# Attention scores as one product of 96 stacked rows per head, with the stacks filled by DMA, on one core

## Chip, cores and metric

The kernel runs on 1 core of one Trainium2 chip. The metric is the device time of the program in microseconds (us). Three executions of the kernel before took 4857.65, 4858.83 and 4860.56 us.

## The reference

Four attention layers are applied to `x` of shape (4, 1024, 512), each as `x = x + layer(layernorm(x))`, with 16 heads of 32 channels and a causal mask:

```python
x = x + attn_a(layernorm(x))  # "squared": (q.k)^2, no softmax; q and k are normed per head; o/(sum+eps); Wo
x = x + ffn(layernorm(x))     # "gated": k and v are one head's share, picked per token by a gate; softmax
x = x + attn_b(layernorm(x))  # "mqa": one k, v for all heads; softmax; output projection with bias
x = x + ffn(layernorm(x))     # "gated" again
# gated:
att = einsum('bhqd,bkd->bhqk', q, k_shared) / sqrt(32)
att = softmax(where(causal, att, -inf)); y = einsum('bhqk,bkd->bhqd', att, v_shared)
```

## The kernel before, in words

There are two acts. The first does the squared layer for the four batch entries, the second the three softmax layers ("soft" in the names of buffers: gated, mqa, gated, each for four entries, so 12 stages). A stage has four phases `ph` of four heads (a head group: 4 x 32 channels on 128 partitions); the first act has 16 phases and the second 48.

A phase makes the scores of its four heads in ten **keys** bursts (`KEY_BURSTS`: keys on partitions, up to 512 queries along the row, the upper triangle left out in blocks of 128) and, in the second act, the scores of the phase that follows in ten **rows** bursts (`ROW_BURSTS`: the same scores with queries on partitions), of which only the row maxima are wanted. The maxima become a shift of the softmax: `mxr` (VectorE and GpSimd), `mxt` (TensorE transposes the maxima to a row, ScalarE takes them out). ScalarE turns the keys bursts into probabilities, GpSimd masks them (`affine_select`) and adds up the unmasked ones, and TensorE multiplies them with the values (`av`) and sums them (`sm`).

Queries and keys are kept as two rounded halves, HIGH and LOW (fp32r), and a score is the sum of three products of 32 rows each (`PAIRS`): high by high, high by low, low by high. The four heads lie in different row quarters of TensorE and their products run side by side, so a part of a burst is 12 matmuls in three groups of four. In the second act a keys part begins with four bf16 matmuls that put the shift into PSUM (line 1107), and a rows part on the diagonal ends with four bf16 matmuls that add the mask (line 1138). VectorE then takes the maximum of two heads in one `reduce_max` (line 885).

Scores live in six PSUM banks as three pairs of banks, used in turn; a burst uses two pairs, one for each two heads. `need_pairs` makes TensorE wait for both pairs of a burst before its first matmul, and both become complete at the burst's end. The other work uses two banks in turn (`work`).

The order of everything is one list of events (`plan`) that all engines walk, each doing its share. `phase` fixes the bursts and the `av`, `sm`, `mxr`, `mxt` events in 20 half steps a phase; `spread` fills the other products in between by their `WEIGHT` and by due times; long ones are halved (`more` events). `q`, `q2`, `k2` are products that make queries and keys, four f32 matmuls by 128 channels (eight instructions in the trace); `kvar` (L1228) is eight small matmuls on the squares of the keys, which GpSimd makes in two instructions (`ksq`, lines 696 and 697) after VectorE has written the LOW half. SyncE issues all DMAs in the list's order.

## Time and profile before

| | us |
|---|---|
| median of 3 runs | 4858.83 |
| the profiled execution's own time | 4860.0 |
| its span | 4858.0 |
| TensorE busy in the span | 4146.2 (85%) |
| VectorE, ScalarE, GpSimd busy | 1919.3, 1600.3, 1585.0 |
| first act, second act (first to last instruction, about) | 0 to 1204, 1204 to 4858 |
| DMA queue of SyncE, share of 16 engines | 7.3% |

The span is the stretch between first and last instruction; the time has about 2 us more. TensorE's busy time is a union of pipelined matmuls, so for the price of a piece of work the start of the next piece is read, not the busy time.

### The profile page before, as it was taken

The numbers are of one execution on the slowest core, as the hardware profiler recorded it, in microseconds if no ns is written. First come the engines' busy times: TensorE is split into PE (matmuls) and PEld (weight loads), VectorE is DVE, ScalarE is ACT, GpSimd is POOL, SyncE is SP. The second block draws the span as 40 slices with busy tenths as digits, with TensorE's granted clock in tenths as the row PEclk, the third lists the DMA queues.
The fourth block names the chain that finished last, engine by engine and source line by source line (L and its number), as shares of the span: only waits on it lengthen the run. The fifth ranks groups of instructions, "written<-read, shape, count | busy, mean of one in ns | idle before, by whom it ended". The sixth has DMA issues, their size and how long they took to land.

```text
span 4858.0 us, 85613 instructions
## 1 busy us (share of the span) xinstructions
PE 4146.2 (85%) x36898; PEld 1987.7 (41%) x36898; DVE 1919.3 (40%) x2850; ACT 1600.3 (33%) x1985; POOL 1585.0 (33%) x1703
## 2 busy tenths in 40 slices
PE   6799898996979889798888888888899897988886
PEld 4344444442434444444443334434444444444443
DVE  1222222222544444444444444344444444444442
ACT  1333333342133233333433333233332333333333
POOL 1322222221133332424443343343333324242343
PEclk8899999998989999999998999999999999999998
DMA  1001001012000100101010010100101001010010
GB/s 59 18 1 36 18 18 36 1 36 88 14 18 1 40 14 1 53 1 36 19 36 18 4 50 1 36 19 18 36 1 36 18 1 53 1 36 18 1 36 29
DMA packets 63442, 116.23 MB, mean 24 GB/s; under 512 B 8673, under 2 KB 9185, under 8 KB 63073
## 3 DMA queue, kind: packets, MB, share of 16 engines
q1 hardware_dynamic: 63072, 110.77, 7.3%
q8 instruction: 298, 4.88, 0.4%
q14 instruction: 72, 0.58, 0.0%
HBM read 77.19 MB, written 33.55 MB: 23 GB/s over the span
## 4 chain that ended last, share of the span: by engine, by line
PE 54%; DVE 8%; POOL 4%; ACT 4%; issue 4%; DMA 1%; POOLq 0%; DVEq 0%; ACTq 0%; SPq 0%
PE banks L1176 11%; PE banks L1078 9%; PE banks L1129 8%; PE banks L1071 7%; PE banks L1111 6%; DVE maxima_soft L885 5%; PE banks L1107 3%; ACT probs_soft L812 3%; POOL full_sum_soft L730 3%; PE banks L1275 2%; PE banks L1138 2%; PE banks L1250 1%; PE banks L1166 1%; PE banks L1185 1%; POOL tiles_soft L710 1%
## 5 line engine op out<-in xcount | busy, mean ns | idle before, releaser
L885 DVE TENSOR_REDUCE maxima_soft<-banks 128x2 f32<-128x1024 f32 (+3 forms) x1152 | 1040.9, 953 | 1120.3 <-PE banks L1138 821.1
L812 ACT ACTIVATE probs_soft<-banks 128x1024 f32<-128x1024 f32 (+1 forms) x960 | 889.6, 978 | 1299.1 <-PE banks L1111 1299.0
L720 POOL TENSOR_SCALAR_AFFINE_SELECT probs_soft<-probs_soft 128x512 f32<-128x512 f32 x384 | 239.0, 634 | 1188.9 <-ACT probs_soft L812 1188.4
L1129 PE MATMUL banks<-k_soft,q_soft 32*128 32x512 f32 (+2 forms) x6912 | 498.9, 391 | 67.5 <-ACT probs_soft L812 66.0
L1111 PE MATMUL banks<-q_soft,k_soft 32*128 32x512 f32 (+2 forms) x6912 | 525.6, 412 | 0.0
L730 POOL TENSOR_TENSOR full_sum_soft<-full_sum_soft,probs_soft 128x2048 f32<-128x2048 f32 x96 | 435.7, 4538 | 251.6 <-ACT probs_soft L812 251.3
L1176 PE MATMUL banks<-probs_soft,v_soft 128*32 128x512 f32 (+3 forms) x4608 | 450.0, 510 | 16.6 <-DVE scaled_out_soft L1022 11.7
L1129 PEld LDWEIGHTS banks<-k_soft,q_soft 32*128 32x128 f32 x6912 | 287.9, 192 | 373.0 <-issue 341.9
L812 ACT ACTIVATE probs_squared<-banks 128x1024 f32<-128x1024 f32 (+1 forms) x320 | 296.5, 978 | 391.5 <-PE banks L1111 305.8
L1107 PE MATMUL banks<-shift_soft,ones 32*128 32x512 bf16 (+2 forms) x2304 | 212.7, 356 | 171.0 <-DVE maxima_soft L885 167.1
L1111 PEld LDWEIGHTS banks<-q_soft,k_soft 32*128 32x128 f32 x6912 | 325.8, 196 | 17.7
L730 POOL TENSOR_TENSOR full_sum_soft<-probs_soft 128x2048 f32<-128x2048 f32 x48 | 217.7, 4536 | 350.0 <-issue 232.7
L1176 PE MATMUL banks<-probs_soft,ones 128*32 128x512 f32 (+3 forms) x3072 | 264.3, 464 | 62.9 <-ACT shift_soft L798 41.5
L1071 PE MATMUL banks<-xnT_soft,g_wq 128*128 128x512 f32 x512 | 249.7, 616 | 11.0 <-DVE q_soft L911 8.6
L1078 PE MATMUL banks<-g_wk,xnT_soft 128*128 128x512 f32 x512 | 255.5, 630 | 3.9 <-ACT y_soft L798 3.6
L1078 PE MATMUL banks<-g_wv,xnT_soft 128*128 128x512 f32 x512 | 247.4, 613 | 13.4 <-DVE sums_soft L985 9.7
L1107 PEld LDWEIGHTS banks<-shift_soft,ones 32*128 32x128 bf16 x2304 | 65.6, 92 | 412.1 <-issue 401.2
L1176 PEld LDWEIGHTS banks<-probs_soft,v_soft 128*32 128x32 f32 x4608 | 124.4, 112 | 260.4 <-issue 215.6
L720 POOL TENSOR_SCALAR_AFFINE_SELECT probs_squared<-probs_squared 128x512 f32<-128x512 f32 x128 | 79.7, 635 | 440.2 <-ACT probs_squared L812 440.2
L1185 PE MATMUL banks<-ident,tiles_soft 128*128 128x128 f32 x384 | 85.0, 365 | 131.4 <-POOL tiles_soft L710 130.7
L1111 PE MATMUL banks<-q_squared,k_squared 32*128 32x512 f32 (+2 forms) x2304 | 158.0, 386 | 22.9 <-ACT probs_squared L812 22.8
L1176 PEld LDWEIGHTS banks<-probs_soft,ones 128*32 128x32 f32 x3072 | 83.3, 112 | 198.9 <-issue 92.2
(160 smaller groups left out, 4751.3 us busy)
## 6 DMA issues: line engine op xcount, KB each, us to landing
tiles_soft<-out SPq DMA_DIRECT2D x96, 256.0 KB, 2.7
rest_soft<-out SPq DMA_DIRECT2D x96, 256.0 KB, 3.0
out<-rest_soft SPq DMA_DIRECT2D x96, 256.0 KB, 2.5
tiles_squared<-in_x SPq DMA_DIRECT2D x32, 256.0 KB, 2.7
rest_squared<-in_x SPq DMA_DIRECT2D x32, 256.0 KB, 2.9
out<-rest_squared SPq DMA_DIRECT2D x32, 256.0 KB, 2.0
raw_wq<-in_squared_wq SPq DMA_DIRECT2D x1, 1024.0 KB, 5.5
raw_wk<-in_squared_wk SPq DMA_DIRECT2D x1, 1024.0 KB, 7.7
```

The source lines that it names most:

```text
L720: ins = pool.affine_select(out=cells, in_=cells, compare_op=ALU.is_ge, fill=0.0, base=0, pattern=[[0, HG], [1, P]], channel_multiplier=-1)
L730: pool.tensor_tensor(m["full_sum"][:], before, slot(ph, n)[:], ALU.add).then_inc(sg.probs_added, 1)
L812: act.activation(slot(ph, n)[:, 2 * a:2 * a + 2, 0:width], score_pair(e, a)[:, :, 0:width], ACT.Exp if soft else ACT.Square, scale=SCALE). ...
L885: ins = dve.reduce_max(m["maxima"][:, ph % 2, 2 * a:2 * a + 2, t, p], score_pair(e, a)[:, :, col:col + P * blocks_seen(t, p, blocks)], AX_X)
L1071: ins = pe.matmul(out, wt[:, kc, cols], m["xnT"][:, kc, CHUNK * c:CHUNK * c + CHUNK], start=(kc == 0), stop=(kc == KC - 1))
L1078: ins = pe.matmul(out, m["xnT"][:, kc, P * t:P * t + P], wt[:, kc, cols], start=(kc == 0), stop=(kc == KC - 1))
L1107: pe.matmul(psum[:, score_bank(e, i), col:col + width], k["ones16"][D * i:D * i + D, :], m["shift"][D * i:D * i + D, ph % 2, c, q0:q0 + wi ...
L1111: ins = pe.matmul(psum[:, score_bank(e, i), col:col + width], k_of(ph)[D * i:D * i + D, a, P * kb:P * kb + P], q_of(ph)[D * i:D * i + D, b ...
L1129: ins = pe.matmul(psum[:, score_bank(e, i), col:col + P * blocks], q_of(ph)[D * i:D * i + D, a, P * t:P * t + P], k_of(ph)[D * i:D * i + D ...
L1138: ins = pe.matmul(psum[:, score_bank(e, i), last - P:last], k["ident16"][:], k["mask"][:], start=False, stop=True)
L1176: ins = pe.matmul(out[D * i:D * i + D, q0:q0 + width], left, slot(ph, n)[:, i, col:col + width], start=(x == 0 and (soft or u == "av" or p ...
L1185: ins = pe.transpose(tile_of(out, kc), tile_of(m["tiles"][:, tile_slot(s, t), :], kc), k["ident"][:])
```

## The change

1. A score is one product. For each head the rows of queries (HIGH, HIGH, LOW) and of keys (HIGH, LOW, HIGH) are stacked to 96 partitions, and one fp32r matmul of 96 rows gives the sum of the three products. In the second act keys bursts have 98 rows: two more rows of queries hold the shift's HIGH and LOW part against two rows of ones of the keys. The matmuls of L1107 and L1138 are gone. A part of a burst is four matmuls, two for each pair of banks, and TensorE waits for one pair at a time (`need_pair`).
2. The stacks are filled by DMA. ScalarE and VectorE write HIGH and LOW of a `q`, `q2` or `k2` into one of two buffers `pair`; SyncE copies them with 12 DMAs of 32 x 512 elements (64 KB) into one of three stacks of 512 columns; the shift takes four DMAs of 2 x 512. In the list these are the events `stack` and `shifted`. Keys of the second act are not copied: they are made four times over already and are written in place. The bf16 split of the maxima in three parts (five GpSimd instructions) becomes an fp32r split in two (two instructions), and the transposes of `mxt` are fp32r matmuls with the identity.
3. The causal mask of row scores is added by VectorE, for one head at a time, in a `tensor_tensor_reduce` that also takes the maximum.
4. The list is made anew: `av` and `sm` are no longer halved and stand at one place each; queries (and keys of the first act) are made later and by halves of the phase (`made`), `kvar` stands right behind `ksq`.

```diff
-PAIRS = [(HIGH, HIGH), (HIGH, LOW), (LOW, HIGH)]
+QUERY_ROWS, KEY_ROWS = (HIGH, HIGH, LOW), (HIGH, LOW, HIGH)
+STACKS = 3
+STACK = 3 * D
-VALUES_AT = {"C": 0, "A": 6, "B": 14}
+VALUES_AT = {"C": 1, "A": 7, "B": 15}
-HALVED = ("av", "sm", "q", "q2", "k2", "v2", "ks", "kall", "vall")
+HALVED = ("q", "q2", "k2", "v2", "ks", "kall", "vall")
 def features(ph):
-    return [(u, ph, c) for c in range(NC) for u in ("q2", "k2", "ksq")] + [("kvar", ph, c) for c in range(NC)] + [("vscale", ph)]
+    made = [[("q2", ph, c), ("qsq", ph, c), ("k2", ph, c), ("ksq", ph, c), ("kvar", ph, c)] for c in range(NC)]
+    return made[0], made[1] + [("vscale", ph)]
@@ phase
-        for u, first in (("av", h), ("sm", h + 2)):
-            pieces = in_halves([(u, of, part)], kinds)
-            for n, event in enumerate(pieces):
-                at[first + n].append(event)
+        at[h].append(("av", of, part))
+        at[h + 1 if part == "B" else h].append(("sm", of, part))
@@ plan, second act
+                return [(queries(kinds[s + g // NG], 4 * s + g)[c], HALVES * (g - 2) + 6 * c, HALVES * (g - 1) - 2 + 6 * c)]
@@ stacked: where the DMAs stand in the list
+        if e[0] in ("q", "q2", "k2"):
+            u, ph, c = e
+            number = NC * ph + c - STACKS
+            old, chunk = divmod(number, NC)
+            waiting.append((("stack", e), ("keys", old, ends[u[0], chunk]) if number >= 0 else None))
+        elif e[0] == "mxt":
+            placed.append(("shifted", e))
+        elif e[0] == "keys":
+            passed.add(e)
+        while waiting and (waiting[0][1] is None or waiting[0][1] in passed):
+            placed.append(waiting.pop(0)[0])
@@ SyncE
+                elif u == "stack":
+                    wait_free(sp, made)
+                    if number >= STACKS:
+                        sp.wait_ge(sg.keys_scored, 2 * (of_kind["keys", old, last] + 1))
+                    for i in range(HG):
+                        for x, a in enumerate(QUERY_ROWS if name[0] == "q" else KEY_ROWS):
+                            sp.dma_start(stack[D * x:D * x + D, number % STACKS, i, :].bitcast(F32),
+                                         pair_of(made)[D * i:D * i + D, a, :].bitcast(F32))\
+                                .then_inc(sg.stacked[moved[made] % 2], DMA)
@@ ScalarE, before it writes HIGH
+                        if moved[e] >= 2:
+                            wait_stack(act, old)
@@ VectorE
+                            if p < t // TPC:
+                                ins = dve.reduce_max(...)
+                                continue
+                            for x in range(2):
+                                scores = score_pair(e, a)[:, x, col:col + width]
+                                ins = dve.tensor_tensor_reduce(scores, scores, k["mask"][:, CHUNK - width:CHUNK], 1.0, MASKED, ALU.add,
+                                                               ALU.max, m["maxima"][:, ph % 2, 2 * a + x, t, p:p + 1])
@@ TensorE, keys (rows are alike)
-                    need_pairs(e)
-                    for kb, q0, width, col in parts:
-                        if soft:
-                            for i in range(HG):
-                                pe.matmul(psum[:, score_bank(e, i), col:col + width], k["ones16"][D * i:D * i + D, :],
-                                          m["shift"][D * i:D * i + D, ph % 2, c, q0:q0 + width], start=True, stop=False)
-                        for x, (a, b) in enumerate(PAIRS):
-                            for i in range(HG):
-                                ins = pe.matmul(...)
+                    rows = STACK + 2 if soft else STACK
+                    for a in range(2):
+                        need_pair(e, a)
+                        for kb, q0, width, col in parts:
+                            for i in (2 * a, 2 * a + 1):
+                                ins = pe.matmul(psum[:, score_bank(e, i), col:col + width], k_stack(ph, i, P * kb, P, rows),
+                                                q_stack(ph, c, i, q0, width, rows), start=True, stop=True)
+                        ins.then_inc(sg.keys_scored, 1)
```

Three places show how the list moves instructions. In these listings an f32 product stands as `x4` where the trace has eight instructions, and the shape is that of the output.

First, TensorE in the first act, where the keys of the second phase (`k2`, s_wk) and their variances (L1228, now L1318) are made between the first bursts. Before:

```order
L1071 MATMUL banks<-xnT_squared,s_wk 128x512 x2
L1111 MATMUL banks<-q_squared,k_squared 128x512 x12
L1176 MATMUL banks<-probs_squared,v_squared 32x512 x4
L1176 MATMUL banks<-probs_squared,v_squared 32x384 x4
L1071 MATMUL banks<-xnT_squared,s_wk 128x512 x2
L1176 MATMUL banks<-probs_squared,v_squared 32x256 x4
L1176 MATMUL banks<-probs_squared,v_squared 32x128 x4
L1228 MATMUL banks<-head_mean,key_square_squared 128x4 x4
```

Of the change:

```order
L1178 MATMUL banks<-xnT_squared,s_wq 128x512 x4
L1215 MATMUL banks<-q_stack_squared,k_stack_squared 128x384 x4
L1178 MATMUL banks<-xnT_squared,s_wk 128x512 x4
L1318 MATMUL banks<-head_mean,key_square_squared 128x4 x4
L1215 MATMUL banks<-q_stack_squared,k_stack_squared 128x256 x8
```

The variances now follow the product of the same keys with nothing on TensorE in between; before, half an `av` stood there (and at other places whole bursts).

Second, TensorE in the second act from the last keys burst of the fifth phase (the two parts 256 wide) over the next rows and keys bursts to the first rows burst of the phase after next. Before:

```order
L1111 MATMUL banks<-q_soft,k_soft 128x256 x12
L1129 MATMUL banks<-k_soft,q_soft 128x512 x12
L1138 MATMUL banks<-mask,ident 128x128 x4
L1107 MATMUL banks<-shift_soft,ones 128x512 x4
L1111 MATMUL banks<-q_soft,k_soft 128x512 x12
L1176 MATMUL banks<-probs_soft,v_soft 32x512 x4
L1176 MATMUL banks<-probs_soft,v_soft 32x384 x4
L1071 MATMUL banks<-xnT_soft,g_wq 128x512 x4
L1176 MATMUL banks<-probs_soft,v_soft 32x256 x4
L1176 MATMUL banks<-probs_soft,v_soft 32x128 x4
L1071 MATMUL banks<-xnT_soft,g_wq 128x512 x4
L1185 MATMUL banks<-ident,tiles_soft 128x128 x8
```

Of the change, down to the same rows burst (L1228, 256 wide) and the `av` behind it:

```order
L1228 MATMUL banks<-k_stack_soft,q_stack_soft 128x512 x4
L1215 MATMUL banks<-q_stack_soft,k_stack_soft 128x256 x8
L1228 MATMUL banks<-k_stack_soft,q_stack_soft 128x512 x4
L1215 MATMUL banks<-q_stack_soft,k_stack_soft 128x512 x4
L1178 MATMUL banks<-xnT_soft,g_wq 128x512 x4
L1228 MATMUL banks<-k_stack_soft,q_stack_soft 128x256 x8
L1266 MATMUL banks<-probs_soft,v_soft 32x512 x4
```

Between the last keys burst and the rows burst of new queries stand two bursts and one product now, and the two `av` pieces have become one behind that rows burst; four bursts follow each other with nothing between.

Third, SyncE in the second act, one phase's worth. Before, it had only the loads and stores of tiles there:

```order
L681 DMA out<-rest_soft 128x512 [waits summed]
L673 DMA rest_soft<-out 128x512 [waits stored0]
L681 DMA out<-rest_soft 128x512 [waits summed]
L673 DMA rest_soft<-out 128x512 [waits stored1]
L681 DMA out<-rest_soft 128x512 [waits summed]
```

Of the change, where no tile is loaded or stored:

```order
L737 DMA q_stack_soft<-shift_soft 2x512 [waits work_free1]
L737 DMA q_stack_soft<-shift_soft 2x512 x3
L730 DMA q_stack_soft<-pair_soft 32x512 [waits keys_scored,work_free0]
L730 DMA q_stack_soft<-pair_soft 32x512 x11
L737 DMA q_stack_soft<-shift_soft 2x512 [waits work_free0]
L737 DMA q_stack_soft<-shift_soft 2x512 x3
L730 DMA q_stack_soft<-pair_soft 32x512 [waits keys_scored,work_free1]
L730 DMA q_stack_soft<-pair_soft 32x512 x11
```

A stack's 12 DMAs wait until the keys bursts that read the stack's former contents have been scored.

## Rows read from the trace of the kernel before

**Rows 1.** Page, part 1: busy us of each engine (share of the span), instructions.
```profile
PE 4146.2 (85%) x36898; PEld 1987.7 (41%) x36898; DVE 1919.3 (40%) x2850; ACT 1600.3 (33%) x1985; POOL 1585.0 (33%) x1703
```
**Rows 2.** Waits of TensorE: who waited for whom, us in total, times, longest.
```profile
PE banks L1107 <- DVE maxima_soft L885: 167.1, 195, 4.7
...
PE banks L1129 <- ACT probs_soft L812: 66.0, 66, 1.3
...
PE banks L1228 <- POOL key_square_squared L697: 31.3, 10, 3.4
```
**Rows 3.** Timeline of TensorE, bursts between other work: start, us, instructions.
```profile
3021.38 0.97 PE L1129 MATMUL banks<-k_soft,q_soft 32*128 32x512 f32 x12
3022.28 1.99 PE L1071 MATMUL banks<-xnT_soft,m_wq 128*128 128x512 f32 x4
3024.19 0.40 PE L1107 MATMUL banks<-shift_soft,ones 32*128 32x512 bf16 x4
...
3025.22 0.66 PE L1250 MATMUL banks<-ident,sums_soft 128*128 128x128 f32 x4
```
**Rows 4.** Timeline of TensorE, narrower parts and the mask.
```profile
1339.70 0.63 PE L1129 MATMUL banks<-k_soft,q_soft 32*128 32x256 f32 x12
1340.26 0.40 PE L1138 MATMUL banks<-mask,ident 128*128 128x128 bf16 x4
...
1354.99 0.80 PE L1129 MATMUL banks<-k_soft,q_soft 32*128 32x384 f32 x12
1355.73 0.40 PE L1138 MATMUL banks<-mask,ident 128*128 128x128 bf16 x4
1356.05 1.93 PE L1176 MATMUL banks<-probs_soft,v_soft 128*32 128x512 f32 x16
...
1362.22 0.29 PE L1107 MATMUL banks<-shift_soft,ones 32*128 32x256 bf16 x4 [1.40 <-DVE maxima_soft L885]
...
1362.70 0.30 PE L1107 MATMUL banks<-shift_soft,ones 32*128 32x256 bf16 x4
```
**Rows 5.** Timeline of TensorE where bursts follow each other, idle time before in brackets.
```profile
1342.64 0.40 PE L1107 MATMUL banks<-shift_soft,ones 32*128 32x512 bf16 x4 [0.31 <-DVE maxima_soft L885]
...
1345.00 0.97 PE L1129 MATMUL banks<-k_soft,q_soft 32*128 32x512 f32 x12 [1.26 <-ACT probs_soft L812]
1347.38 0.40 PE L1107 MATMUL banks<-shift_soft,ones 32*128 32x512 bf16 x4 [1.41 <-DVE maxima_soft L885]
```
**Rows 6.** Timeline of TensorE in the first act: f32 products of 128 rows, then variances.
```profile
78.41 3.60 PE L1071 MATMUL banks<-xnT_squared,s_wq 128*128 128x512 f32 x8
81.84 3.60 PE L1071 MATMUL banks<-xnT_squared,s_wk 128*128 128x512 f32 x8
85.27 0.95 PE L1228 MATMUL banks<-head_mean,key_square_squared 128*128 128x4 f32 x8
89.54 1.23 PE L1228 MATMUL banks<-head_mean,key_square_squared 128*128 128x4 f32 x8 [3.32 <-POOL key_square_squared L697]
```
**Rows 7.** Line 1129, weight loads: duration ns min/median/max.
```profile
L1129 PEld LDWEIGHTS banks<-k_soft,q_soft x6912: 180/183/334, 1266.4 to 4781.3; 32*128 32x128 f32 x198
```
**Rows 8.** VectorE's groups by form: xcount, busy us, mean ns of one.
```profile
L885 DVE TENSOR_REDUCE maxima_soft<-banks 128x2 f32<-128x1024 f32 x576 | 678.5, 1220 | 508.8 <-PE banks L1129 298.5 <-PE banks L1138 210.1
...
L985 DVE TENSOR_TENSOR sums_soft<-banks,sums_soft 128x512 f32<-128x512 f32 x48 | 32.9, 685 | 59.0 <-PE banks L1176 59.0
```
**Rows 9.** Timeline of SyncE's queue, DMAs issued one behind the other.
```profile
8.14 0.42 SPq L426 DMA_DIRECT2D gamma<-in_squared_gamma  x1
8.60 0.42 SPq L427 DMA_DIRECT2D beta<-in_squared_beta  x1
```
**Rows 10.** DMA issues: KB each, median us from issue to landing.
```profile
tiles_soft<-out SPq DMA_DIRECT2D x96, 256.0 KB, 2.7
...
gamma<-in_squared_gamma SPq DMA_DIRECT2D x4, 0.1 KB, 1.6
```
**Rows 11.** Windows, the second act: us, busy of PE, PEld, DVE, ACT, POOL, granted clock, DMA share.
```profile
1204.00:4858.00 3654.00, 3124.71 (x29728) 1487.43 (x29728) 1628.88 (x2432) 1197.64 (x1496) 1279.01 (x1346) 0.94 0.07 22
```

292 lines of the change are left out of this document (169 added, 123 removed).

## Prediction, made blind

> **What bounds the kernel now.** The page's first part is read first: TensorE is busy 85% of the span and no other engine is busy more than 40% [rows 1]. So a change counts by what it does to TensorE's own time and to what TensorE waits for. TensorE's waits come next. Two groups hold what the change is about: 167.1 us in 195 waits of keys bursts for VectorE's maxima, and 66.0 us in 66 waits of rows bursts for ScalarE's probabilities, 233 us together; the variances of the first act wait 31.3 us in 10 waits [rows 2]. The timeline shows where these come from: where bursts follow each other, a rows burst is followed by 1.41 us of idle time, the keys burst behind it by 1.26 us, and a period of both takes 4.74 us (1342.64 to 1347.38), of which TensorE works 2.0 [rows 5]. The cause is in the code: both pairs of a burst end together, and the next burst wants the first of them read out, 1.22 us on VectorE [rows 8].
>
> **Score products.** Prices are start to start of the next piece, so entry and exit are in them. A keys part 512 wide takes 1.03 us (3024.19 to 3025.22), a rows part 0.90 (3021.38 to 3022.28) [rows 3]. A rows part 384 wide takes 0.74, 256 wide 0.56, the mask behind a part 0.32, a keys part 256 wide 0.48 (1362.22 to 1362.70) [rows 4]; a keys part 384 wide is put between, 0.76. A phase of the second act has 6 parts of 512, 2 of 384 and 4 of 256 for keys, the same for rows, and 8 masks: keys 6x1.03 + 2x0.76 + 4x0.48 = 9.6; rows 6x0.90 + 2x0.74 + 4x0.56 + 8x0.32 = 11.7; together 21.3 us.
>
> After the change a part is four matmuls of 96 or 98 rows that go one behind the other. No such fp32r matmul is in the trace; the nearest are the f32 products of 128 rows: 3.43 us for eight instructions of 512 columns [rows 6], 0.43 each, which is twice 512 columns at 2.4 GHz, so 0.215 for one pass. (From 256 to 512 columns the four rounded matmuls side by side, in three groups, grow by 0.90 - 0.56 = 0.34 us for 768 columns, which also is a column per cycle [rows 3, 4].) So 0.86 us for a part of 512, 0.65 for 384, 0.44 for 256 (0.11 each, a little above the 256 columns' 0.107). The weight load is the open cost: a load of 128 fp32 columns shows 0.183 us [rows 7]. Lower bound: it hides behind the matmul ahead, as it does in the f32 products, eight loads in 3.43 us without a gap. Upper bound: the whole 0.183 is laid bare at every one of 48 x 96 + 16 x 48 = 5376 new matmuls. I take the lower, since those products also use all rows. A phase's keys and rows then take 2 x (6x0.86 + 2x0.65 + 4x0.44) = 16.4 us, and 0.1 us of entry behind each of some four `av` and `sm`: 16.8. Gain 4.5 us a phase, 48 phases: **-216**. In the first act, with three groups and no shift (9.1 as the rows without mask) against 8.2: 16 phases, **-14**.
>
> The Trainium skill, "TensorE: Matmul & The Clock Gate", Part 3, "The mechanism", says that a weight load overlaps matmuls in flight only where its row group differs. The f32 products contradict it here. By that rule the new matmuls would pay the load each, which is the upper bound above and a rival below.
>
> **`av` and `sm` in one piece.** Four f32 instructions between bursts take 1.91 us (3022.28 to 3024.19) [rows 3], 0.48 each against 0.43 in a run [rows 6]: some 0.19 for the two ends of a piece. Five pieces fewer in each of 48 phases and six in each of 16 are 336; as `av` pieces have another shape, I take 0.12: **-40**.
>
> **Waits for a pair.** In the order of before, 209 of the second act's 950 steps between bursts hold under 1 us of other TensorE work; 233 us are 1.1 each. In the new order 433 do, since `av`, `sm` and halved products now stand in lumps. But a matmul pair now waits only for the pair three uses back, so a run of bursts goes at VectorE's pace: two pairs are 2.44 us of maxima [rows 8], against 1.72 us of matmuls, 0.36 lost a step; with mask two reads of one head cost 2 x 0.685 by the nearest elementwise row [rows 8], against 1.22: 0.5 a step. 433 x 0.45 = 195: **-38**. The first act has 42 keys bursts without work between against 12, each short by ScalarE's pace: **+10**. Bounds for `tensor_tensor_reduce`, which the trace doesn't show: from 0.685 a head to the sum of both passes, some 1.37.
>
> **Stacks.** SyncE issues a DMA every 0.46 us [rows 9]: 12 take 5.6 us. Landing is 1.6 us for 0.1 KB and 2.7 for 256 KB [rows 10]; 64 KB take 2.0 or so. So a stack stands 7.7 us after its start. Its start is set by the three stacks: the queries of chunk 0 of phase p go where chunk 1 of phase p-2 lay, free after its keys burst 9, and rows burst 0 wants them after one rows and one keys burst. Going through the new order with the prices above, TensorE has 1.7 to 10.3 us of work in that gap, under 7.7 in 39 of 46 phases, short by 79 us in all. The same for chunk 1 (free after keys burst 2, wanted by rows burst 3): 37 of 47 short, 92 us. The shift now goes ScalarE (0.6), four DMAs (1.8), landing (2.0), 4.6 us with signals, with 2.8 us of work ahead of keys burst 3 in the poorest phases: 24 short, 37 us. Sum 208; part of it falls where TensorE would wait for VectorE anyway, and VectorE catches up in it. I take **+130** (bounds 60 and 208). ScalarE, too, waits for a stack before it writes the buffer again, and holds up probabilities; it is inside that sum.
>
> **Variances.** From the end of the key product (85.27) to the variance that waits for its squares (89.54) are 4.27 us [rows 6]: HIGH, LOW and two GpSimd instructions. In the new order 26 of 32 variances have no work, or not enough, between: 26 x 4.0 = 104, less the 31.3 of before: **+72**. Behind it on TensorE stand the next bursts, and ScalarE starves with them.
>
> **Small.** The shift's matmuls in fp32r instead of bf16, 96 x 0.1: **+10**. Clock: the granted clock of the second act is 0.94 [rows 11], so it already falls to 1.2 GHz at times; the long waits of the first act make more of that, the short ones of rows 5 fewer: **+20**.
>
> **Sum.** -216 - 14 - 40 - 38 + 10 + 130 + 72 + 10 + 20 = -66. The profiled execution took 4860.0, 1.2 above the median of 4858.8; 4860 - 66 = 4794, and I put the price of the exits of products between bursts, now of the same shape as their neighbours, on the side of gain: **4788 us**.
>
> **Rivals.**
> - *The waits shrink more than I grant.* Runs of bursts at 2.6 us a period instead of 4.74 keep the clock at 2.4 GHz, and stack waits fall together with VectorE's: stacks +60, clock -30: 4788 - 70 - 50 = 4670. For it: VectorE idle 509 us before its widest maxima [rows 8]. Against: twice as many bare steps. Chance 0.24.
> - *Stacks come later, and it ends slower.* The place is rows bursts 0 and 3 of every phase. If a stack needs 9.5 us instead of 7.7 (issue 0.6 a DMA, or landing nearer 4 us because 12 transfers queue), each of some 85 short gaps loses 1.8 us more: +150, 4940. It decides from about 0.8 us more per stack. For it: several DMAs in flight are the rule here and the issue rows had small ones behind each other [rows 9]; against: 24 packets of 2 KB an engine are little. Chance 0.20.
> - *VectorE's masked maximum costs both passes.* 10240 columns of heads a phase at 0.7 us per 512 are +11 us of VectorE on 34 (1629 us in 48 phases [rows 11]). VectorE would be at 62%; in runs of bursts a masked step loses 1.4 us more, about 110 steps: +150, 4940. Chance 0.08.
> - *Weight loads bare*: 5376 x 0.183 = +984, of which some 180 would lie in waits: about 5590. Chance 0.05, since [rows 6] speak against it.
> - *Nothing to measure*: the planner's lumps and waits eat the gain, 4850 to 4868. Chance 0.06.
>
> **Numbers.** My own case (4730 to 4845) has 0.37. Faster by over 0.2% (about 10 us, what a measurement can tell from no change): 0.37 + 0.24 = 0.61. Within: 0.06. Slower: 0.20 + 0.08 + 0.05 = 0.33. The range reaches from the first rival, 4665, to just over the two at 4940: 4665 to 4965.
>
> **What would show it.** The score lines' matmuls 0.215 apart at 512 columns (wrong: 0.3 or more). Periods near 2.6 us in runs. Waits of TensorE for the stack DMAs at the first and fourth rows burst, 1 to 3 us each, and some 100 us of waits of L1318 for GpSimd. Masked maxima near 0.7 us a head. Landing of the last of 12 DMAs under 2.5 us. Wrong above all would be the walk through the order, which adds up waits that in truth overlap.

## The result, and the profile after

The changed kernel takes 5012.49 us (median of 4 executions, 5010.23 to 5016.56) against 4858.24 for the kernel before beside it: ratio 1.0311, 95% interval 1.029 to 1.0331. It is 3.1% slower. The forecast was 4788, with a range up to 4965: wrong in sign and outside its range.

The page of the changed kernel, parts 1 and 4: busy us of each engine, and the shares of the chain that ended last.

```profile
PE 4095.3 (82%) x22306; PEld 2189.8 (44%) x22306; DVE 2045.4 (41%) x5156; ACT 1602.0 (32%) x1985; POOL 1512.0 (30%) x1414
...
PE 37%; SPq 12%; POOL 7%; DMA 5%; DVE 5%; issue 3%; ACT 3%; POOLq 0%; ACTq 0%; DVEq 0%
```

TensorE works 51 us less than in [rows 1], in a span that is 150 us longer. What is new is SyncE's queue: 12% of the chain is time in which it issues DMAs.

TensorE's waits in the changed kernel, us in total, times, longest:

```profile
PE banks L1275 <- POOL tiles_soft L783: 190.8, 75, 30.2
PE banks L1228 <- DMA q_stack_soft<-pair_soft: 185.1, 66, 7.0
PE banks L1318 <- POOL key_square_squared L769: 132.2, 31, 6.7
PE banks L1275 <- POOL tiles_squared L783: 77.8, 32, 14.1
PE banks L1215 <- DVE maxima_soft L976: 41.0, 65, 5.8
PE banks L1215 <- DVE maxima_soft L981: 33.8, 42, 7.6
...
PE banks L1228 <- DVE maxima_soft L976: 21.8, 55, 0.4
PE banks L1215 <- DMA q_stack_soft<-shift_soft: 16.0, 19, 3.5
...
PE banks L1228 <- DVE maxima_soft L981: 11.6, 30, 0.5
```

The 233 us for maxima and probabilities in [rows 2] have shrunk to 108 for maxima. In their place stand 185 us for the stacks' DMAs, 132 for the squares of the variances (31.3 in [rows 2]), and more for normed tiles.

SyncE's queue, timeline, with the shift's DMAs and a stack ahead of three tile loads:

```profile
3028.54 2.48 SPq L737 DMA_DIRECT2D q_stack_soft<-shift_soft  x4
3031.34 7.50 SPq L730 DMA_DIRECT2D q_stack_soft<-pair_soft  x12
3038.93 1.50 SPq L716 DMA_DIRECT2D tiles_soft<-out  x3
```

Twelve DMAs take 7.50 us, 0.625 each, where [rows 9] gave 0.46. The four of the shift, only 2 x 512 elements each, take 2.48 us, 0.62 each; the three tile loads of 256 KB take 1.50, 0.50 each. The first DMA of the stack goes out once VectorE has written the LOW half (3031.82), and the chain of waits shows what follows: issue after issue (0.59 and 0.04 between), the landing of the last one, and TensorE.

```profile
3030.34 0.70 ACT pair_soft L907
3031.06 0.76 DVE pair_soft L1014
3031.92 0.58 SPq L730
...
3037.61 0.59 SPq L730
3038.24 1.98 DMA q_stack_soft<-pair_soft
3040.26 1.20 PE banks L1228 x4
```

The landing of 1.98 us is counted from the start of the last issue (3038.24) and so holds that issue's 0.6 us. The stack stands 8.9 us after the first issue begins (3031.34 to 3040.22).

TensorE's timeline shows the same wait, behind a product that ended early.

```profile
3034.00 3.60 PE L1178 MATMUL banks<-xnT_soft,m_wq 128*128 128x512 f32 x8
3040.26 1.20 PE L1228 MATMUL banks<-k_stack_soft,q_stack_soft 96*128 96x512 f32 x4 [2.67 <-DMA q_stack_soft<-pair_soft]
```

TensorE, timeline, a run of bursts with nothing between (answers to [rows 5]):

```profile
1537.95 1.20 PE L1228 MATMUL banks<-k_stack_soft,q_stack_soft 96*128 96x512 f32 x4 [0.39 <-DVE maxima_soft L976]
1538.98 0.71 PE L1215 MATMUL banks<-q_stack_soft,k_stack_soft 98*128 98x512 f32 x2
1540.00 0.73 PE L1215 MATMUL banks<-q_stack_soft,k_stack_soft 98*128 98x512 f32 x2 [0.30 <-DVE maxima_soft L976]
1541.13 0.96 PE L1228 MATMUL banks<-k_stack_soft,q_stack_soft 96*128 96x384 f32 x4 [0.40 <-DVE maxima_soft L976]
```

A period takes 3.2 us here (1537.95 to 1541.13) against 4.74 in [rows 5], and 0.3 and 0.4 of it are idle; the forecast said 2.6. Two score matmuls of 512 columns last 0.73 from first start to last end and four last 1.20, so they are (1.20 - 0.73) / 2 = 0.235 us apart: the weight load is hidden, at 9% more than the 0.215 of the forecast. Each part pays for its entry besides: from the start of a part of 512 to the start of the next are 1.03 us (1537.95 to 1538.98) and not 0.86.

VectorE by form, xcount, busy us, mean ns (answers to [rows 8]):

```profile
L976 DVE TENSOR_REDUCE maxima_soft<-banks 128x2 f32<-128x1024 f32 x384 | 452.3, 1220 | 352.0 <-PE banks L1228 350.1
L981 DVE CUSTOM_DVE_ANT_0 banks<-banks,mask 128x512 f32<-128x512 f32 x384 | 253.8, 723 | 73.5 <-PE banks L1228 73.2
L981 DVE DVE_READ_ACCUMULATOR2_ANT maxima_soft<- 128x1 f32 x1536 | 219.7, 143 | 0.2
```

The masked maximum of a head is two instructions, 723 and 143 ns at 512 columns, 0.87 us together.

The DMA issues of the page: count, KB each, median us to landing (answers to [rows 10]).

```profile
q_stack_soft<-pair_soft SPq DMA_DIRECT2D x1152, 64.0 KB, 2.0
```

The first act: a variance right behind its key product waits 4.12 us (timeline of TensorE).

```profile
127.96 1.84 PE L1318 MATMUL banks<-head_mean,key_square_squared 128*128 128x4 f32 x8 [4.12 <-POOL key_square_squared L769]
```

The window behind it (columns as in [rows 11]) has a granted clock of 0.50, which is 1.2 GHz:

```profile
128.00:132.00 4.00, 4.00 (x18) 3.87 (x19) 0.43 (x2) 1.10 (x2) 0.00 (x0) 0.50 0.47 109
```

Window over the second act of the changed kernel: us, busy of PE, PEld, DVE, ACT, POOL, granted clock, DMA share (answers to [rows 11]).

```profile
1350.00:5007.00 3657.00, 3018.91 (x16677) 1620.95 (x16675) 1752.86 (x4739) 1204.64 (x1496) 1206.01 (x1059) 0.91 0.16 44
```

The clock of the second act is 0.91, against 0.94 in [rows 11]; over the whole span it is 0.905, against 0.938. The matmuls of the first act's scores run from 115.0 to 1313.5 us where before they ran from 125.5 to 1141.6: 182 us of the loss lie in the first act. In the second the scores' matmuls run from 1448.4 to 4969.6 where before they ran from 1266.4 to 4819.0, a gain of 31.

### The profile page after: what moved, and what is told of

The parts are those of the page before. It is cut to its first block, busy times and chain, and to the rows that moved or that the text cites. A ratio compares the mean times of both kernels' runs of the same rounds, so it can differ in the third digit from the quotient of the medians.

```text
span 5007.6 us, 59884 instructions
## 1 busy us (share of the span) xinstructions
PE 4095.3 (82%) x22306; PEld 2189.8 (44%) x22306; DVE 2045.4 (41%) x5156; ACT 1602.0 (32%) x1985; POOL 1512.0 (30%) x1414
## 4 chain that ended last, share of the span: by engine, by line
PE 37%; SPq 12%; POOL 7%; DMA 5%; DVE 5%; issue 3%; ACT 3%; POOLq 0%; ACTq 0%; DVEq 0%
PE banks L1266 12%; SPq L730 10%; PE banks L1185 6%; PE banks L1228 5%; POOL full_sum_soft L803 5%; PE banks L1178 4%; PE banks L1215 4%; DMA q_stack_soft<-pair_soft 3%; ACT probs_soft L882 2%; PE banks L1366 2%; DVE maxima_soft L976 2%; DMA tiles_soft<-out 2%; SPq L737 1%; PE banks L1256 1%; POOL tiles_soft L783 1%
## 5 line engine op out<-in xcount | busy, mean ns | idle before, releaser
L981 DVE CUSTOM_DVE_ANT_0 banks<-banks,mask 128x128 f32<-128x128 f32 (+3 forms) x1536 | 703.6, 526 | 428.6 <-PE banks L1228 428.3
L1228 PE MATMUL banks<-k_stack_soft,q_stack_soft 96*128 96x512 f32 (+2 forms) x2304 | 630.9, 405 | 220.1 <-DMA q_stack_soft<-pair_soft 185.1
L1215 PE MATMUL banks<-q_stack_soft,k_stack_soft 98*128 98x512 f32 (+2 forms) x2304 | 636.9, 395 | 96.5 <-DVE maxima_soft L976 41.0
L976 DVE TENSOR_REDUCE maxima_soft<-banks 128x2 f32<-128x1024 f32 x384 | 452.3, 1220 | 352.0 <-PE banks L1228 350.1
L1228 PEld LDWEIGHTS banks<-k_stack_soft,q_stack_soft 96*128 96x128 f32 x2304 | 387.5, 201 | 447.6 <-DMA q_stack_soft<-pair_soft 241.8
L1215 PEld LDWEIGHTS banks<-q_stack_soft,k_stack_soft 98*128 98x128 f32 x2304 | 371.0, 192 | 322.1 <-issue 127.0
L803 POOL TENSOR_TENSOR full_sum_soft<-full_sum_soft,probs_soft 128x2048 f32<-128x2048 f32 x96 | 437.1, 4553 | 38.8 <-ACT probs_soft L882 34.1
L1275 PE MATMUL banks<-ident,tiles_soft 128*128 128x128 f32 x384 | 95.0, 399 | 194.6 <-POOL tiles_soft L783 190.8
L1215 PE MATMUL banks<-q_stack_squared,k_stack_squared 96*128 96x512 f32 (+2 forms) x768 | 221.3, 413 | 17.2 <-ACT probs_squared L882 15.0
L868 ACT ACTIVATE y_soft<-banks 128x512 f32<-128x512 f32 x96 | 57.4, 598 | 537.9 <-PE banks L1266 537.9
L1266 PE MATMUL banks<-probs_soft,ones 128*32 128x512 f32 (+3 forms) x3072 | 225.8, 435 | 0.0
L981 DVE DVE_READ_ACCUMULATOR2_ANT maxima_soft<- 128x1 f32 x1536 | 219.7, 143 | 0.2
```

Of the source, the lines that this page charges most:

```text
L803: pool.tensor_tensor(m["full_sum"][:], before, slot(ph, n)[:], ALU.add).then_inc(sg.probs_added, 1)
L976: ins = dve.reduce_max(m["maxima"][:, ph % 2, 2 * a:2 * a + 2, t, p], score_pair(e, a)[:, :, col:col + width], AX_X)
L981: ins = dve.tensor_tensor_reduce(scores, scores, k["mask"][:, CHUNK - width:CHUNK], 1.0, MASKED, ALU.add, ALU.max, m["maxima"][:, ph % 2, ...
L1215: ins = pe.matmul(psum[:, score_bank(e, i), col:col + width], k_stack(ph, i, P * kb, P, rows), q_stack(ph, c, i, q0, width, rows), start=T ...
L1228: ins = pe.matmul(psum[:, score_bank(e, i), col:col + P * blocks], q_stack(ph, t // TPC, i, P * (t % TPC), P, STACK), k_stack(ph, i, CHUNK ...
L1266: ins = pe.matmul(out[D * i:D * i + D, q0:q0 + width], left, slot(ph, n)[:, i, col:col + width], start=(x == 0 and (soft or u == "av" or p ...
```

## The experiments

Each run was timed beside the kernel before on the same chip, whose medians were 4861 to 4863 us. All medians are of 4 executions but one, as said. The clock is the mean granted clock of the profiled execution (0.938 for the kernel before).

| run | us | ratio to before | 95% interval | clock |
|---|---|---|---|---|
| changed kernel | 5012.5 | 1.0311 | 1.0290 to 1.0331 | 0.905 |
| kvar_late | 4901.1 | 1.0078 | 1.0051 to 1.0104 | 0.906 |
| three_dmas | 4679.6 | 0.9625 | 0.9611 to 0.9639 | 0.925 |
| loads_early | 4995.2 | 1.0272 | 1.0254 to 1.0290 | 0.907 |
| both_pairs | 5178.7 | 1.0648 | 1.0630 to 1.0665 | 0.878 |
| two_queues (10 executions) | 4847.3 | 0.9972 | 0.9962 to 0.9982 | 0.911 |
| no_mask | 5022.5 | 1.0329 | 1.0311 to 1.0346 | 0.903 |
| before_vmask | 4833.2 | 0.9941 | 0.9924 to 0.9958 | 0.931 |
| late_early_two | 4698.1 | 0.9665 | 0.9643 to 0.9687 | 0.926 |
| small_dmas | 4992.0 | 1.0267 | 1.0251 to 1.0283 | 0.908 |
| three_late | 4530.0 | 0.9319 | 0.9304 to 0.9334 | 0.936 |
| values_halved | 4915.7 | 1.0118 | 1.0100 to 1.0136 | 0.912 |
| best_halved | 4757.5 | 0.9788 | 0.9772 to 0.9803 | 0.924 |
| second_act_two | 4609.7 | 0.9477 | 0.9461 to 0.9493 | 0.929 |
| three_late_pairs | 4818.2 | 0.9908 | 0.9893 to 0.9922 | 0.897 |
| three_late_halved | 4571.7 | 0.9397 | 0.9383 to 0.9411 | 0.935 |
| second_act_two_high | 4602.1 | 0.9461 | 0.9447 to 0.9475 | 0.932 |

### What the stacks cost

**three_dmas**, a stack with 3 of its 12 DMAs:

```diff
-                    for i in range(HG):
+                    for i in range(1):
                         for x, a in enumerate(QUERY_ROWS if name[0] == "q" else KEY_ROWS):
...
-        return m["q"][0:rows, (NC * ph + c) % STACKS, i, first:first + width]
+        return m["q"][0:rows, (NC * ph + c) % STACKS, 0, first:first + width]
```

> The changed kernel with 3 of the 12 DMAs of a stack: only head 0 is copied, and the four heads of a phase all read head 0's stack (the other heads' scores are left out of the computation). Theory: a stack is late because SyncE issues its 12 DMAs 0.62 us apart, 7.5 us, and tile loads stand behind it; with 1.9 us of issue a stack stands some 4 us after its start, TensorE's waits for stack DMAs (185 us in 66) fall under 40, those of normed tiles behind the queue by 50, and the time by 150 to 200 us, to 4810 to 4860. Rival: the waits for stacks lie where TensorE would wait for VectorE or ScalarE anyway, and the time falls by under 60 us.

4679.6, 333 us less than the changed kernel, nearly twice what the theory gave. Its waits (TensorE, us in total, times, longest):

```profile
PE banks L1275 <- POOL tiles_soft L783: 157.7, 75, 30.5
...
PE banks L1275 <- POOL tiles_squared L783: 47.6, 32, 6.7
...
PE banks L1228 <- DMA q_stack_soft<-pair_soft: 8.0, 6, 2.1
```

A stack in SyncE's timeline:

```profile
2831.30 1.82 SPq L730 DMA_DIRECT2D q_stack_soft<-pair_soft  x3
```

The stack waits are gone (185.1 to 8.0), and 63 us of the waits for normed tiles with them: together 240 us. Most of the rest is TensorE's busy time, which falls by 81 us (4095.3 to 4014.0) for the same 22306 instructions, at a clock of 0.925 and not 0.905:

```profile
PE 4014.0 (86%) x22306; PEld 2172.7 (46%) x22306; DVE 2040.0 (44%) x5156; ACT 1602.3 (34%) x1985; POOL 1512.2 (32%) x1414
```

The scores of the second act take 288 us less (3233.0 against 3521.2) and begin 35 us sooner (1413.4 against 1448.4). The rival that hides the stacks in other waits falls.

**small_dmas**, twelve DMAs that carry an eighth of the bytes:

```diff
-                            sp.dma_start(stack[D * x:D * x + D, number % STACKS, i, :].bitcast(F32),
-                                         pair_of(made)[D * i:D * i + D, a, :].bitcast(F32))\
+                            some = CHUNK if number < STACKS else 64
+                            sp.dma_start(stack[D * x:D * x + D, number % STACKS, i, 0:some].bitcast(F32),
+                                         pair_of(made)[D * i:D * i + D, a, 0:some].bitcast(F32))\
```

> The changed kernel with all twelve DMAs of a stack, but from the fourth stack of each act on only 64 of the 512 columns are copied (the other columns keep the first stacks' data, so most scores are left out of the computation). Theory: the cost is that one queue issues twelve DMAs 0.62 us apart, whatever they carry: the pitch stays 0.5 us or more and the time stays above 4950. Rival: the pitch follows the bytes in flight (64 KB each): it falls to 0.3 us or less, and the time to that of three DMAs, 4680 to 4750.

4992.0. SyncE's timeline shows the same pitch:

```profile
3017.45 7.50 SPq L731 DMA_DIRECT2D q_stack_soft<-pair_soft  x12
```

The page's DMA issues show a landing 0.3 us sooner:

```profile
q_stack_soft<-pair_soft SPq DMA_DIRECT2D x1116, 8.0 KB, 1.7
```

So the price is that of the number of DMAs in one queue: 20 of the 333 us hang on the bytes.

**two_queues**, heads 2 and 3 issued by ScalarE behind the same waits:

```diff
-                    for i in range(HG):
+                    for i in range(HG // 2):
...
+                elif u == "stack":
+                    made = e[1]
+                    wait_free(act, made)
...
+                    for i in range(HG // 2, HG):
+                        for x, a in enumerate(QUERY_ROWS if name[0] == "q" else KEY_ROWS):
+                            act.dma_start(m[name[0]][D * x:D * x + D, number % STACKS, i, :].bitcast(F32),
```

> The changed kernel with half of a stack's DMAs (heads 2 and 3) issued by ScalarE at the same place of the list, behind the same waits; SyncE issues the other six. Theory: what costs is the time in which one queue issues twelve DMAs, 7.5 us; with two queues side by side it is 3.8 us, and about half of the 333 us that leaving out nine DMAs gave comes back, less some ScalarE time: 4840 to 4890. TensorE's waits for q_stack fall from 185 us to 60 or so. Rival 1: the transfers themselves are slow or collide, whatever queue they come from: within 30 us of 5012. Rival 2: ScalarE loses the six issues, 96 times 3.7 us, ahead of probabilities that TensorE waits for: slower than 5012.

4847.3, 165 us less, half of the 333. ScalarE's timeline shows its own six, in this stack at 0.67 us each, while SyncE issues the other six (from 2902.21, 3.71 us):

```profile
2902.23 4.02 ACTq L896 DMA_DIRECT2D q_stack_soft<-pair_soft  x6
```

The gain lies in the second act alone. Its keys matmuls run from 1573.0 to 4808.8 where the changed kernel's run from 1491.8 to 4969.6: 3235.8 against 3477.8, 242 us less. The first act's run from 117.4 to 1398.5, 83 us more: there the squares wait for what ScalarE does late, as TensorE's waits show.

```profile
PE banks L1333 <- POOL key_square_squared L769: 195.9, 31, 11.7
...
PE banks L1243 <- DMA q_stack_soft<-pair_soft: 31.7, 17, 3.4
```

**loads_early**, the first three loads of a stage 8 keys bursts ahead in the list, the reloads 4:

```diff
-    return stacked(two_banks(events), soft)
+    return earlier_loads(stacked(two_banks(events), soft))
```

> The changed kernel with the first three tile loads of each stage put 8 keys bursts ahead in the list, and the first three reloads of the residual 4 bursts, so that SyncE issues them ahead of stacks and not behind. Theory: waits of L1275 for normed tiles (190.8 us in 75 and 77.8 in 32) fall by some 80 us, of which 60 to 100 reach the end: about 4930. Rival: the other five loads of a stage, each issued behind its ln, and the chain of statistics behind them set these waits: under 25 us.

4995.2, 17 us less. The waits for normed tiles fall by 21 us in the first act (77.8 to 57.0) and hardly in the second (190.8 to 186.8). The rival holds for the first three loads of a stage. Yet three_dmas took 63 us of these waits away, so something of the stacks does reach them; that it is the other five loads, which still stand behind stacks in the queue, was not tried.

### The variances

**kvar_late**:

```diff
+def later_variances(events, kinds):
...
+        if e[0] == "kvar":
+            held.append([e, 4.0])
+            continue
+        placed.append(e)
+        for h in held:
+            h[1] -= weight(e, kinds)
```

> The changed kernel with each kvar (and the vscale behind it) moved later in the list by 4 us of TensorE work by the planner's weights; nothing else. Theory: the variances' waits for GpSimd's squares are a cost of their own, 132.2 us in 31 waits, and the first act's clock falls in them: the waits go to under 30 us, the time falls by 100 to 130 us to about 4895, the first act alone gets shorter. Rival: the wait is only handed on to the next wait behind it (stack or probabilities): under 50 us.

4901.1, 111 us less. The first act's score matmuls now run from 109.8 to 1199.4, 109 us less than in the changed kernel, and of the waits for squares this is left:

```profile
PE banks L1339 <- POOL key_square_squared L790: 13.8, 6, 4.5
```

The waits fall by 118 us, and those for the first act's normed tiles rise by 16 (77.8 to 93.3). Over the first act's scores TensorE's busy time falls by 34 us (1033.4 to 999.8) and the clock goes from 0.88 to 0.89, so a part of the gain is the clock's, as the theory had it.

### Pair waits, mask and halves

**both_pairs**:

```diff
+                    need_pair(e, 0)
+                    need_pair(e, 1)
                     for a in range(2):
-                        need_pair(e, a)
```

> The changed kernel with TensorE waiting for both pairs of banks before a burst, as before the change; nothing else. Theory: waiting pair by pair was worth, in the 433 steps with little other work between, some 0.65 us each, 280 us, and 30 us in the first act: slower by 200 to 310 us, about 5250. Rival: VectorE and ScalarE set the pace in those runs either way, since a pair's reading starts when the pair is complete in both: slower by under 80 us.

5178.7, 166 us more: between the two theories. The waits for maxima and probabilities rise by 182 us, those for stacks fall by 65 (120.1 left), the clock falls to 0.878. All of TensorE's idle time together, span less busy time, grows by 36 us only (912.3 to 948.4), and its busy time by 138 (4095.3 to 4233.6). TensorE's waits:

```profile
PE banks L1216 <- DVE maxima_soft L981: 94.5, 94, 8.2
PE banks L1216 <- DVE maxima_soft L976: 83.0, 82, 6.1
PE banks L1230 <- ACT probs_soft L882: 81.2, 138, 1.1
```

**no_mask**, one reduce_max of two heads also on the diagonal:

```diff
-                            if p < t // TPC:
+                            if p <= t // TPC:
```

> The changed kernel without the causal mask in the row maxima: the two tensor_tensor_reduce of a pair become one reduce_max of two heads, as for unmasked parts (the mask of the row maxima is left out of the computation). Theory: a masked pair costs VectorE 1.29 us against 1.22 in one reduce_max, so it is nearly free: 0 to 30 us faster. Rival: the accumulator read behind each of the 1536 instructions (143 ns, 220 us in all) holds up bursts: 60 us or more faster.

5022.5, by its interval no faster than with the mask. VectorE is busy 130 us less (2045.4 to 1915.7) and the waits for maxima fall by 20 (to 88.5), but those for stacks rise by 22 (185.1 to 207.5). The mask on VectorE costs the changed kernel no time; what it would cost with the stacks out of the way was not tried.

**before_vmask**, part 3 alone in the kernel before:

```diff
-                        diagonal = p == t // TPC
+                        diagonal = False
...
+                                ins = dve.tensor_tensor_reduce(scores, scores, k["mask"][:, CHUNK - width:CHUNK], 1.0, MASKED, ALU.add,
+                                                               ALU.max, m["maxima"][:, ph % 2, 2 * a + x, t, p:p + 1])
```

> The kernel before with part 3 of the change alone: the four bf16 mask matmuls behind each diagonal rows part are gone, and VectorE adds the mask in tensor_tensor_reduce, head by head. Theory: TensorE loses 48 x 8 pieces of 0.32 us, 123 us, and VectorE's reading gets 0.1 us a pair longer in steps that wait for it; 70 to 120 us faster than before, 4740 to 4790. Rival: in the dry runs of bursts TensorE waits for VectorE and the saved matmuls only lengthen the wait: under 30 us faster.

4833.2, 30 us less (0.6%), far under the theory's 70 and just the rival's. TensorE's busy time falls by 105 us and its idle time rises by 75, 53 of them for maxima; the clock goes from 0.938 to 0.931. Those waits:

```profile
PE banks L1114 <- DVE maxima_soft L892: 126.1, 135, 5.2
PE banks L1114 <- DVE maxima_soft L887: 94.4, 88, 4.4
```

**values_halved**, `av` and `sm` in halves at the half steps of before (the places of `sm` and the weights of both in the list, not shown, go back with them):

```diff
-VALUES_AT = {"C": 1, "A": 7, "B": 15}
+VALUES_AT = {"C": 0, "A": 6, "B": 14}
-HALVED = ("q", "q2", "k2", "v2", "ks", "kall", "vall")
+HALVED = ("av", "sm", "q", "q2", "k2", "v2", "ks", "kall", "vall")
```

> The changed kernel with av and sm in halves again, at the half steps where they stood before the change (the rest of the list follows from that). Forecast's term: undoing this costs 40 us, about 5050. Theory: halves of other work between bursts fill steps that are bare now, as the pair waits and the clock show (0.905), and that is worth more than the 0.12 us of a piece's ends: 20 to 80 us faster, 4930 to 4990.

4915.7, 97 us less: the forecast's term has the wrong sign here. The waits for maxima fall from 108 us to 44, those for normed tiles by 37, and the stack waits are 55 us shorter:

```profile
PE banks L1231 <- DMA q_stack_soft<-pair_soft: 130.1, 66, 6.9
```

### Versions

**late_early_two**, the three edits together:

> The changed kernel with the variances later, the loads earlier and the stacks' DMAs on two queues, all three. If the three are independent the gains add up: 111 + 17 + about 130, 4750 to 4770, which would be faster than before the change. If they share waits, or ScalarE's issues cost more in the first act, over 4820.

4698.1: the three gains by themselves add up to 293, together they give 314.

**best_halved**, that version with halves:

> The version with later variances, earlier loads and stacks on two queues (4698), with av and sm in halves as well. If the halves pay by filling bare steps, 20 to 80 us faster, 4620 to 4680; if the added piece ends cost, about 4740.

4757.5, 59 us more; of the two cases the second, about 4740, came out. Halving does fill bare steps here too: the waits for maxima fall from 113 us to 59. But TensorE's idle time as a whole falls by 9 us only (690.1 to 680.9), since other waits grow, and its busy time rises by 60 (4007.7 to 4067.5).

### What is left of the sum

**three_late**, the edits of three_dmas and kvar_late:

> The changed kernel with three of twelve DMAs a stack (all heads read head 0's stack; the other heads' scores are left out of the computation) and the variances later in the list. It shows what the rest of the change is worth once the two disputed costs are gone. By the forecast's own terms without those two, 4794 - 130 - 72 = 4592; by the two runs apart, if they add, 4680 - 111 = 4569. If another term is badly mis-sized (products, halves, clock), it comes out over 4640.

4530.0, 6.8% faster than before. The two edits do not simply add: together they give 482 us and apart 333 + 111 = 444. Later variances are worth 150 us once the nine DMAs are gone (4679.6 to 4530.0). TensorE by the page:

```profile
PE 3952.8 (87%) x22306; PEld 2143.0 (47%) x22306; DVE 2041.2 (45%) x5156; ACT 1602.8 (35%) x1985; POOL 1515.1 (33%) x1414
```

**three_late_pairs** and **three_late_halved** are this kernel with the edits of both_pairs and values_halved:

> The version with three of twelve DMAs and later variances (4530 us; the scores of three heads are left out of the computation), with TensorE waiting for both pairs again. It prices the pair waits without stacks. The forecast gave them 38 us less than before the change and hence, against waits of 433 steps at 1.1 us, some 280 us for this undoing: 4810. With stacks it was 166 us (5179 against 5012); if the stacks hid part of it, more than 166 here; if it is the clock that pays, the granted clock falls from 0.936 to about 0.90.

4818.2, 288 us more, and a clock of 0.897. The number is the forecast's (some 280), but not what it is made of. That was 280 us of waits; here TensorE's idle time grows by 122 us (575.0 to 697.3) and its busy time, for the same instructions, by 164:

```profile
PE 4116.4 (86%) x22306; PEld 2253.1 (47%) x22306; DVE 2040.1 (42%) x5156; ACT 1594.8 (33%) x1985; POOL 1511.1 (31%) x1414
```

> The version with three of twelve DMAs and later variances (4530 us; the scores of three heads are left out of the computation), with av and sm in halves. With stacks in the way halving was worth 97 us (4916 against 5012), in the version with two queues it cost 59 (4757 against 4698). Theory: halving shifts other work into the steps before the stack waits and so hides stacks, and by itself it costs the ends of pieces, the forecast's 40 us: 4560 to 4590 here. Rival: it fills bare steps in any case: under 4500.

4571.7, 42 us more: with the stacks' DMAs cut to three the halves cost what the forecast said, 40. The waits for maxima fall here as well, from 108.5 us to 48, of which the largest is

```profile
PE banks L1239 <- DVE maxima_soft L1005: 27.2, 38, 2.4
```

but the idle time as a whole falls by 4 us only (575.0 to 571.2), and the busy time rises by 50 (3952.8 to 4002.7).

**second_act_two**:

```diff
-                    for i in range(HG // 2):
+                    for i in range(HG // 2 if soft else HG):
...
-                elif u == "stack":
+                elif u == "stack" and soft:
```

> The version of 4698 us (later variances, earlier loads, two queues) with the second queue in the second act alone; in the first act SyncE issues all twelve DMAs again. With two queues everywhere the first act's scores took 1137.7 us (111.8 to 1249.5), with variances later alone 1089.6 (109.8 to 1199.4). If ScalarE's issues are what costs there: about 50 us faster, 4640 to 4660. Rival: the first act is then held by stacks instead, and it stays within 15 us of 4698.

4609.7, 88 us less than 4698.1. The first act's score matmuls run from 111.7 to 1157.2, 1045.5 us against 1137.7, so ScalarE's share of the issues was what held that act. The gain is larger than the 50 us expected.

**second_act_two_high**:

```diff
-                    wait_free(sp, made)
+                    sp.wait_ge(sg.high_ready, high_parts[made])
...
+                    for i, x, a in sorted(copies, key=lambda copy: copy[2]):
+                        if (i, a) == (0, LOW):
+                            wait_free(sp, made)
```

> The version with the second queue in the second act alone, with SyncE issuing the copies of the HIGH half first, as soon as ScalarE has written it, and those of the LOW half behind them. In the first act a stack starts with VectorE's LOW half and in the second with the old stack's last use, so only the first act can gain: 0 to 30 us faster than the version without. Rival: in the first act ScalarE and VectorE are waited for anyway: within 5 us.

4602.1, 7.6 us less; the first act is no shorter (110.4 to 1156.2), so the reason given for a gain fails, and its size is at the edge of what is told apart. At 4602.1 it is the fastest version that leaves nothing out, 5.4% faster than the kernel before.

## Why the forecast was wrong

**The step that failed** is the stack's time: "SyncE issues a DMA every 0.46 us" and "12 take 5.6 us", hence "a stack stands 7.7 us after its start". The pitch is 0.625 us, 12 take 7.50 us, and a stack stands 8.9 us after its start (3031.34 to 3040.22), 1.2 us more. That is the side of the second rival (chance 0.20), which named an issue of 0.6 a DMA and "decides from about 0.8 us more per stack". Its 9.5 us, like the forecast's 7.7, counts the last issue twice: the landing of [rows 10] is from issue to landing. I had the pitch from loads of 0.1 KB and took it as the pitch of any. It is not the bytes that make the difference (0.625 at 64 KB and at 8 KB, 0.62 at the shift's 4 KB, 0.50 at a tile load's 256 KB); what does was not tried.

**The term for stacks** was +130 with an upper bound of 208. three_dmas prices nine of twelve DMAs at 333 us. Even the rival's 130 + 150 = 280 falls short. TensorE's waits for stacks and shift came to 201 us (185.1 + 16.0), near the 208 of the walk through the order, so the discount to 130, for gaps that overlap with VectorE, was not due. Two things were not in the walk: 63 us of waits for normed tiles, and the 81 us that TensorE's busy time grows by at the lower clock (0.905 against 0.925). An estimate of what the pitch alone did: the scores of the second act take 3233.0 us where a stack stands 3.2 us after its start (three_dmas, the last of three issues and its landing), 3279.0 where it stands after some 5.3 (two_queues, the last of six) and 3521.2 where it stands after 8.9. On a straight line between the last two, 7.7 us would have cost 207 us more than three_dmas, and the 1.2 us beyond it 81. So the pitch is one part of the miss and the price put on a late stack another. The landing, 2.0 us, was right.

**Variances**, +72: 111 by kvar_late. The mechanism was foreseen and its size was not: 31 waits of 4.3 us are 132 against 31.3, 101 more and not 72. With the stacks out of the way the edit is worth 150.

**What remains of the sum without these two** is 4794 - 130 - 72 = 4592; three_late has 4530, 62 less. By the pages TensorE's busy time falls by 193 us from the kernel before to three_late, and the terms for work had 260 (216 + 14 + 40 - 10): 67 too much. Its idle time falls by 137 (711.8 to 575.0), and the pair waits had 28: 109 too little. The clock cost nothing there and had 20. That makes the 62. By terms:
- *Halves*, -40: 42 by three_late_halved. Right in size. In the changed kernel the same edit has the other sign, -97; there the waits for stacks and normed tiles fall with it by 92 us, which three_late_halved had little of to lose. That it moves work into the stacks' gaps fits this and was not tried by itself. With two queues, where only 33 us of stack waits were left, it costs 59.
- *Pair waits*: undoing them costs 288 us where the prices gave 280, by luck, as the idle time grows by 122 only. The net -38 failed: I left 195 us of waits in the second act, and three_late has 40.4 + 34.4 + 20.8 + 12.9 = 108.5 there.
- *Score products*, -230: the matmuls are 0.235 apart and not 0.215, 9% of 16.4 us a phase, so about 70 us of gain less in the second act; the entry of each part (1.03 us for 0.86, in the run of bursts above) makes it more. The 193 us above are of all work together, and how they divide among scores, products and halves stays open. The mechanism (no bare weight load) was right, the rival at 5590 wrong. The Trainium skill's rule of row groups, as the forecast gave it ("TensorE: Matmul & The Clock Gate", Part 3, "The mechanism"), is contradicted here: matmuls of 96 and 98 rows overlap their 0.19 us loads. The same section of the Trainium skill also lets a load go ahead when it targets the background weight buffer, and with that these matmuls agree.
- *Clock*, +20: in three_late 0.936 against 0.938, so nearly nothing. In the changed kernel it is 0.905, and TensorE is busy 142 us longer than in three_late (4095.3 against 3952.8) for the same 22306 instructions. Part of that (the 81 us above) is in the price of the stacks.
- Not in the sum at all: the waits of `av` and `sm` for free work banks, 41.5 us for ScalarE alone before, have all but gone in three_late, and waits for normed tiles have grown by some 52 us (157.8 + 63.3 against 130.7 + 38.8).

TensorE's waits in three_late, from which these numbers are:

```profile
PE banks L1296 <- POOL tiles_soft L804: 157.8, 75, 30.8
PE banks L1296 <- POOL tiles_squared L804: 63.3, 29, 9.2
PE banks L1236 <- DVE maxima_soft L997: 40.4, 63, 5.8
PE banks L1236 <- DVE maxima_soft L1002: 34.4, 43, 7.9
...
PE banks L1249 <- DVE maxima_soft L997: 20.8, 53, 0.4
...
PE banks L1249 <- DVE maxima_soft L1002: 12.9, 32, 0.7
```

None of these items was tried by itself; that they sum to the 62 us is bookkeeping from the pages.

**VectorE's mask** cost no time in the changed kernel; its rival (0.08) is out by no_mask, though a head of 512 columns takes 0.87 us and not 0.685. Taken alone (before_vmask) it gains 30 us and not 123: of the 105 us that TensorE's busy time falls by, 75 come back as idle time.

## What to carry to other kernels

Price a fan-out of DMAs by their number in the queue, from DMAs of the same form, and count everything that stands behind them in that queue; the bytes hardly mattered. Where a chain of small transfers is late, splitting the issue over a second queue gave half of it back here, but only where that engine's own work is not waited for. When a wait is removed or added, ask for the clock too: of the price of the nine DMAs a quarter was TensorE's busy time (81 of 324 us), and of the pair waits more than half (164 of 286). And an edit that reorders work (the halves) must be tried with the other defects mended, since its sign hung on them.

## What the runs showed of the hardware

- SBUF to SBUF DMAs are issued every 0.62 to 0.63 us on SyncE's queue: 12 of 64 KB in 7.50 us, 12 of 8 KB in 7.50 us (small_dmas), four of 4 KB in 2.48 us. Loads of 256 KB went out every 0.50 us, those of 0.1 KB in [rows 9] every 0.46. On ScalarE's queue six took 4.02 us, beside SyncE's six in 3.71 (two_queues).
- fp32r matmuls of 96 or 98 rows and 512 columns follow each other every 0.235 us, with loads of 0.19 us hidden; a part of four, with its entry, takes 1.03 us.
- `tensor_tensor_reduce` is two instructions on VectorE, 723 and 143 ns at 512 columns. Two such heads are 1.73 us against 1.22 for one `reduce_max` of both, yet the kernel was no faster without them (no_mask).
- The granted clock falls from 0.936 to 0.897 from three_late to three_late_pairs, with the same instructions and 122 us more idle time. The amount of idle time alone does not set it: the kernel before is idle for 711.8 us at 0.938, three_late_pairs for 697.3 at 0.897. What does stays open.
